# Gathers moved from the start of a stage into the stage before it, with weights and small engine steps re-ordered, in a graph network on one core

## Time and profile before

| | us |
|---|---|
| median of 3 runs | 6474.08 |
| lowest and highest | 6468.80, 6482.52 |
| the profiled execution | 6475.1 |
| its span on the core | 6473.4 |
| busy: PE, DVE, ACT, POOL | 3347.9, 4132.0, 1517.7, 4139.2 |
| mean granted clock of TensorE | 0.675 of full |

### The profile page before, as it was taken

One profiled execution on the slowest core, in us unless ns is written; L12 is line 12 of the kernel. 1 busy time (PEld: TensorE's weight loads), 2 busy tenths in 40 slices (PEclk: granted clock), 3 DMA queues, 4 the chain that ended last, 5 costly groups with the idle time before them and its releaser, 6 DMA issues. The chain is left out here.

```text
span 6473.4 us, 52111 instructions
## 1 busy us (share of the span) xinstructions
PE 3347.9 (52%) x13821; PEld 2034.4 (31%) x13823; DVE 4132.0 (64%) x5381; ACT 1517.7 (23%) x3187; POOL 4139.2 (64%) x4234
## 2 busy tenths in 40 slices
PE   3576777755777776573333333333334333333363
PEld 2355555544555555341111111111111111111231
DVE  5577777766777777565555554555554555555597
ACT  0122222201222221012223322222232233222221
POOL 0477777726777775127777776777775777777230
PEclk7677777876776777785555656556656555666686
DMA  0576666627666665463333332333332333333341
GB/s 22 147 205 194 194 197 199 192 78 203 197 200 196 195 196 148 178 193 98 105 105 105 107 105 85 106 105 105 104 106 87 101 105 107 106 105 102 131 153 61
DMA packets 541084, 877.90 MB, mean 136 GB/s; under 512 B 85205, under 2 KB 383297, under 8 KB 532622
## 3 DMA queue, kind: packets, MB, share of 16 engines
q0 software_dynamic: 167776, 479.21, 25.7%
q1 hardware_dynamic: 373032, 395.35, 19.0%
HBM read 553.75 MB, written 320.47 MB: 135 GB/s over the span
## 5 line engine op out<-in xcount | busy, mean ns | idle before, releaser
L1219 POOL DMA_INDIRECT big<-h_tab,big x2352 | 2219.5, 944 | 812.1 <-issue 812.1
L1265 PE MATMUL psum<-big 128*128 128x512 f32 x1176 | 1086.6, 1079 | 1779.2 <-ACT big L1242 1779.0
L633 POOL DMA_INDIRECT big<-kv_tab,big x1664 | 1645.3, 989 | 532.6 <-issue 498.3
L1302 DVE TENSOR_TENSOR psum<-psum,big 128x1024 f32<-128x1024 f32 x294 | 555.7, 1890 | 1337.7 <-DMA big<-h_tab,big 1337.7
L1265 PEld LDWEIGHTS psum<-big 128*128 128x128 f32 x1176 | 342.7, 322 | 2358.6 <-ACT big L1242 2055.1
L1236 ACT COPY big<-big 128x1024 f32<-128x1024 f32 x294 | 563.5, 1917 | 2097.0 <-DVE big L1285 2097.0
L762 PE MATMUL psum<-big 128*128 128x136 f32 x3328 | 691.6, 358 | 502.7 <-DVE big L820 316.2
L762 PEld LDWEIGHTS psum<-big 128*128 128x128 f32 x3328 | 592.5, 250 | 598.4 <-issue 569.7
L672 ACT COPY big<-psum 125x128 f32<-125x128 f32 x1408 | 375.8, 267 | 1478.2 <-PE psum L718 1394.1
L1285 DVE TENSOR_TENSOR_SCAN big<-big,psum 128x1024 f32<-128x1024 bf16 x294 | 669.0, 2275 | 0.1
L710 PE MATMUL psum<-big 128*128 x4992 | 581.2, 263 | 105.3 <-DVE big L791 105.0
(11 more groups left out here) (391 smaller groups left out, 3315.8 us busy)
## 6 DMA issues: line engine op xcount, KB each, us to landing
run_tab<-big SPq DMA_DIRECT2D x294, 512.0 KB, 2.7
snap_tab<-big SPq DMA_DIRECT2D x176, 448.0 KB
item_tab<-big SPq DMA_DIRECT2D x208, 272.0 KB
big<-loc_tab SPq DMA_DIRECT2D x104, 512.0 KB, 4.6
big<-h_tab,big POOLq DMA_INDIRECT x2352, 2.5
big<-kv_tab,big POOLq DMA_INDIRECT x1664, 3.4
snap_tab<-big SPq DMA_DIRECT2D x176, 52.0 KB
kv_tab<-big SPq DMA_DIRECT2D x12, 512.0 KB, 2.6
```

Source lines behind the costliest of these rows:

```text
L633: nc.gpsimd.indirect_dma_start(out=kv[:, b % SLOTS, k, :], out_offset=None, in_=kv_tab, in_offset=bass.IndirectOffsetOnAxis(ap=src_item[:, ...
L1219: nc.gpsimd.indirect_dma_start(out=got[j % RING][:, k * D:(k + 1) * D], out_offset=None, in_=h_tab, in_offset=bass.IndirectOffsetOnAxis(ap ...
L1265: ins_ = nc.tensor.matmul(bank[2 * (j % DEEP) + k][:, :], ea_T[j % DEEP], w_blocks[:, k * 512:(k + 1) * 512], start=True, stop=True)
L1302: nc.vector.tensor_tensor(by_feature(msg[j % DEEP]), by_feature(msg[j % DEEP]), got[j % RING].rearrange("p (t f) -> p f t", f=D), ALU.add) ...
```

## The change

It touches the first seven stages of the list above:

- `node_linear` and `node_math` are replaced by one stage per layer, `conv_linear`: keys and values are multiplied for all tiles first, two tiles to a bank, then queries and roots; the weights have two semaphores. In the second layer the joins of `node_math` run in it quad by quad, ACT applying the ReLU on its copy. When the table is written, POOL issues the gathers of batches 0 to 2 (`FIRST`) there.
- `conv_finish` makes its one-hots ahead of DVE's first wait (an index tile that they need is made at the end of `conv_edges`), and adds `x` to `skip` in the second layer; `norm_linear` (1) has no L1453 any more.
- `norm_linear` (1) and (3) have POOL issue the first 8 count rows (`EARLY`); `by_src` begins with the ninth. In all three, ACT takes the root of a quad ahead of the next quad's squares, and DVE scales the variance ahead of the next join.
- The four loads of `norm_linear` (2) are issued in `by_src` on `x` instead. Some buffers change places for this.

The diff, cut to its core, each level of indentation shortened to one space:

```diff
+  kv_ring = area(B1, 4 * SLOTS * 2 * D).rearrange("p (b k c) -> p b k c", k=4, c=2 * D)
+  def kv_rows(b, slot_in):
+   for k in range(4):
+    nc.gpsimd.indirect_dma_start(
+     out=kv_ring[:, b % SLOTS, k, :], out_offset=None, in_=kv_tab,
+     in_offset=bass.IndirectOffsetOnAxis(ap=src_item[:, 4 * b + k:4 * b + k + 1], axis=0)).then_inc(slot_in[b % SLOTS], 16)
...
+      for b in range(FIRST, BATCHES):
        if b >= SLOTS:
         pool.wait_ge(va_done, b - SLOTS + 1)
-       for k in range(4):
-        nc.gpsimd.indirect_dma_start(
-         out=kv[:, b % SLOTS, k, :], out_offset=None, in_=kv_tab,
-         in_offset=bass.IndirectOffsetOnAxis(ap=src_item[:, 4 * b + k:4 * b + k + 1], axis=0)).then_inc(slot_in[b % SLOTS], 16)
+       kv_rows(b, slot_in)
...
+      if layer == 1:
+       nc.vector.tensor_tensor(skip[:, :], skip[:, :], x[:, :], ALU.add)
       link_(nc.vector.memset(gT, 0.0))
+      side_hots(0)
+      side_hots(1)
       dve.wait_ge(from_pe, 1)
...
       nc.vector.engine_nop().then_inc(to_act, 1)
-      dve.wait_ge(made, 1)
-      side_hots(0)
       dve.wait_ge(from_act, 2)
...
       nc.vector.engine_nop().then_inc(to_pe, 1)
-      side_hots(1)
       dve.wait_ge(from_pe, 2)
...
+  FIRST = 3
+  def conv_linear(layer, source, slot_in, scale_of=None, joined=None):
+   groups = [[(lo, min(lo + 2, hi)) for lo in range(first_, hi, 2)] for first_, hi in QUADS]
+   pairs = [p for g in groups for p in g]
...
+     ph, "kv_w_in", "qs_w_in", "node_step", "joined_done", "tr_done", "copied", "mm_done", "evac", "tab_out")
...
     with nc.Block() as block:
+     @block.gpsimd
+     def _(pool):
+      pool.wait_ge(tab_out, 16 * len(QUADS))
+      for b in range(FIRST):
+       kv_rows(b, slot_in)
      @block.sync
      def _(sp):
...
+      for k, (n, loaded) in enumerate((("k", kv_in), ("v", kv_in), ("q", qs_in), ("s", qs_in))):
+       sp.dma_start(wgt[:, k * D:(k + 1) * D], a[f"L0_{n}_w{layer}"]).then_inc(loaded, 16)
+       sp.dma_start(bias[:, k * D:(k + 1) * D], a[f"L0_{n}_b{layer}"].to_broadcast([P, D])).then_inc(loaded, 16)
...
+      for g, (lo, hi) in enumerate(QUADS):
+       seen += len(groups[g])
+       sp.wait_ge(evac, seen)
+       sp.dma_start(table(kv_tab)[:, lo:hi, :], kv_n3[:, lo:hi, :]).then_inc(tab_out, 16)
+      sp.wait_ge(qs_in, 16 * 4)
...
+       nc.scalar.activation(turned[:, lo * D:hi * D], bank[g % 2][:, 0:(hi - lo) * D], ACT.Relu if layer else ACT.Copy).then_inc(copied, 1)
      @block.tensor
      def _(pe):
       def turn(g):
        lo, hi = QUADS[g]
+       if joined is not None:
+        pe.wait_ge(joined_done, g + 1)
        later(pe, copied, g - 1)
        for t in range(lo, hi):
         ins_ = nc.tensor.transpose(bank[g % 2][:, (t - lo) * P:(t - lo + 1) * P], source[:, t * D:(t + 1) * D], ident[:, :])
        ins_.then_inc(tr_done, 1)
+      def products(q, at):
+       lo, hi = pairs[q % many]
+       if q >= 6:
+        pe.wait_ge(evac, outs_at(q - 6))
+       for t in range(lo, hi):
+        ins_ = nc.tensor.matmul(bank[2 + q % 6][:, (t - lo) * 2 * D:(t - lo + 1) * 2 * D], turned[:, t * D:(t + 1) * D], wgt[:, at:at + 2 * D], start=True, stop=True)
+       ins_.then_inc(mm_done, 1)
       turn(0)
...
+      pe.wait_ge(kv_in, 16 * 4)
+      q = 0
+      for g in range(len(QUADS)):
        if g + 1 < len(QUADS):
         turn(g + 1)
        pe.wait_ge(copied, g + 1)
...
+       for _ in groups[g]:
+        products(q, 0)
+        q += 1
+      pe.wait_ge(qs_in, 16 * 4)
+      for q in range(many, 2 * many):
+       products(q, 2 * D)
      @block.vector
      def _(dve):
...
+      link = Chain(dve, step)
+      def kv_out(q):
+       lo, hi = pairs[q]
+       dve.wait_ge(mm_done, q + 1)
...
+      if scale_of is not None:
+       scale_of(link)
+      q = 0
+      for g in range(len(QUADS) + 2):
+       if joined is not None and g < len(QUADS):
+        joined(link, *QUADS[g], work3)
+        nc.vector.engine_nop().then_inc(joined_done, 1)
+       if g == 1:
+        dve.wait_ge(kv_in, 16 * 4)
+       for _ in groups[g - 2] if g >= 2 else ():
+        kv_out(q)
+        q += 1
+      dve.wait_ge(qs_in, 16 * 4)
+      for q in range(many, 2 * many):
+       lo, hi = pairs[q - many]
+       dve.wait_ge(mm_done, q + 1)
...
+       for dst, at in ((q_n3, 0), (skip3, D)):
+        nc.vector.tensor_tensor(dst[:, lo:hi, :], out[:, :, at:at + D], bias[:, 2 * D + at:3 * D + at].unsqueeze(1).to_broadcast([P, hi - lo, D]), ALU.add).then_inc(evac, 1)
...
+  R, EARLY = 9, 8
+  counts = [area(k * NP, NP) for k in range(R)]
+  def count_rows(v, cin):
+   at = NT + v if v < 5 else v - 5
+   nc.gpsimd.indirect_dma_start(out=counts[v % R], out_offset=None, in_=snap_tab,
+          in_offset=bass.IndirectOffsetOnAxis(ap=own_at[:, at:at + 1], axis=0)).then_inc(cin[v % R], 16)
...
+     @block.gpsimd
+     def _(pool):
+      for v in range(EARLY if counts_to else 0):
+       count_rows(v, counts_to)
      @block.sync
      def _(sp):
...
       for n in range(last + 1):
+       if n > 0:
+        lo, hi = QUADS[n - 1]
+        act.wait_ge(varied, n)
+        nc.scalar.activation(root[:, lo:hi], var[:, lo:hi], ACT.Sqrt).then_inc(rooted, 1)
        if n < last:
         lo, hi = QUADS[n]
         act.wait_ge(centre, n + 1)
...
        if n > 0:
         lo, hi = QUADS[n - 1]
-        act.wait_ge(varied, n)
-        nc.scalar.activation(root[:, lo:hi], var[:, lo:hi], ACT.Sqrt).then_inc(rooted, 1)
...
       for n in range(last + 3):
+       if 0 < n <= last:
+        spread_of(n - 1)
        if n < last:
         centred(n)
-       if 0 < n <= last:
-        spread_of(n - 1)
        if n >= 3:
         product_out(n - 3)
        if 0 < n <= last:
...
+  conv_edges(1, conv_in)
+  conv_finish(1)
+  norm_linear([(wgt[:, 0:D], a["L1_WT"][0:D, :]), (wgt[:, D:2 * D], a["L1_WT"][D:2 * D, :]), (bias[:, 0:D], a["L1_b"].to_broadcast([P, D]))],
+     node_sums, work3, shares, counts_to=mean_in)
...
     with nc.Block() as block:
      @block.gpsimd
      def _(pool):
-      for v in range(NT + 5):
+      for v in range(EARLY, NT + 5):
        later(pool, mm_done, v - R + 1)
-       at = NT + v if v < 5 else v - 5
-       nc.gpsimd.indirect_dma_start(out=counts[v % R], out_offset=None, in_=snap_tab,
-              in_offset=bass.IndirectOffsetOnAxis(ap=own_at[:, at:at + 1], axis=0)).then_inc(cin[v % R], 16)
+       count_rows(v, cin)
      @block.sync
...
-       sp.wait_ge(we_in, 16 * 10)
+       sp.dma_start(wgt[:, 0:D], a["L2_W_enc"]).then_inc(we_in, 16)
+       sp.dma_start(bias[:, 0:D], a["L2_b_enc"].to_broadcast([P, D])).then_inc(we_in, 16)
+       sp.dma_start(bn[:, :], a["L2_bn"]).then_inc(we_in, 16)
+       sp.dma_start(epsb[:, 0:3], a["L2_eps"].to_broadcast([P, 3])).then_inc(we_in, 16)
+       sp.wait_ge(we_in, 16 * 14)
      @block.vector
...
-  norm_linear([(wgt[:, 0:D], a["L2_W_enc"]), (bias[:, 0:D], a["L2_b_enc"].to_broadcast([P, D])),
-        (bn[:, :], a["L2_bn"]), (epsb[:, 0:3], a["L2_eps"].to_broadcast([P, 3]))], plus_x,
+  norm_linear([], plus_x,
...
+  gat_in = dma_sems(*[f"gat_in{k}" for k in range(R)])
   norm_linear([(wgt[:, 0:D], a["L3_WT"]), (bias[:, 0:D], a["L3_b"].to_broadcast([P, D])),
         (a12[:, 0:D], a["L3_a"][:, 0:D].to_broadcast([P, D])), (a12[:, D:], a["L3_a"][:, D:].to_broadcast([P, D])),
-        (lnwb[:, 0:D], a["L3_ln_w"].to_broadcast([P, D])), (lnwb[:, D:], a["L3_ln_b"].to_broadcast([P, D]))], plus_x, work3)
-  hh = area(0, NPF)
+        (lnwb[:, 0:D], a["L3_ln_w"].to_broadcast([P, D])), (lnwb[:, D:], a["L3_ln_b"].to_broadcast([P, D]))], plus_x, work3, counts_to=gat_in)
+  hh = area(8 * NPF, NPF)
```

## The result

The changed kernel takes **6399.12 us** (median of 4 runs, 6395.10 to 6406.73) beside 6473.39 for the kernel before: a ratio of 0.9885, 95% interval [0.9873, 0.9898]. The forecast was 6406, 6378 to 6436. The profiled execution of the changed kernel took 6406.73, its span is 6404.6, 68.8 shorter than the span before; -68.3 was forecast on that scale. On this pair of executions the sum is right to half a microsecond; its terms are not.

A forecast was written before the change was run, and what follows sets the result against it. No engine was taken to bound the kernel throughout; stages were read singly, waits for counts opening both by_src the main prize. Terms of -85.3 plus 17 gave -68.3 from 6475.1, or 6406 us against the median; range 6378 to 6436.

The forecast's parts named there:

- the start of both by_src: by_src on x and on skip: count rows arrive during the stage before, removing DVE's first waits; -31.3 and -22.9 us.
- the encoder's loads: norm_linear (2): loads land under by_src, so PE's 17.13 us wait goes; with the root's order -17.4 us.
- The first attention stage: First layer's attention stage: PE bounds keys and values, table lands at 206.4, stage ends with POOL's twelfth gather; +3.5 us.
- The second stage: Second layer's attention stage: joins go quad by quad, then table and gathers; -6.4 us, bounds -8 and -2.
- POOL's early gathers: Attention stages: 12 gathers at 1.25 us each, 15.1 us; no gain counted in conv_edges.
- the wait of 12.12: conv_edges, batch 14: POOL waits 12.12 us for a slot that DVE's work frees, so earlier gathers only wait longer.
- the rival with 4%: conv_edges: POOL is the bound after all, early gathers count in full, -15 us per layer, 6375 us; 4%.
- the new wait in norm_linear (3): norm_linear (3): six weight loads queue with the count rows, PE waits at its first product; +17 us, +10.5 to +23.
- No hold: norm_linear (3): small loads slip through within 11 us, stage takes 31.3 us; -85 in all, 6389 us; 25%.
- conv_edges and the gine layers, put at 0: conv_edges and three GINE layers: no step touched, so no change counted, though moved buffers and DMA traffic might lengthen conv_edges.
- The rule of the Trainium skill: norm_linear (3): DMA engines alternate queues, draining one whole packet each turn; by it the hold nears the lower end, +12.
- The clock rival: by_src on x: TensorE's clock stays at 1.2 GHz after idle, 25 steps 5.4 us longer, +135, 6541 us; 3%.

The follow-up runs named there:

- experiment 3: Changed kernel with no count rows issued before by_src (0 in both norms): 6444.07 us, +45 against the changed kernel.
- experiment 5: Changed kernel with the encoder's four loads issued in norm_linear (2) again: 7434.66 us on a slower chip; norm_linear (2) 49.5 instead of 33.6.
- experiment 7: Changed kernel with the root behind the next quad's squares and variance scaling behind the next join again, all three norms: 7444.51 us on a slower chip.
- experiment 1: Changed kernel without gathers ahead of conv_edges (FIRST = 0): 6379.21 us, 0.9849 to the kernel before.
- experiments 9 to 12: Three variants of the changed kernel and, third, that kernel again, on a chip where the kernel before takes 7600.99: 7493.79, 7483.72, 7486.93, 7482.23 us.
- experiment 8: Changed kernel with norm_linear (3)'s six loads issued only after the first count row landed: 7440.00 us on a slower chip; stage 60.5 instead of 39.1.
- 4: Changed kernel without gathers ahead of conv_edges, and with five count rows in norm_linear (3), three in the scores' stage: 6376.59 us, 0.9848 to the kernel before.
- 6: Changed kernel with seven count rows in norm_linear (1), five in (3), none in the scores' stage: 7421.28 us on a slower chip.
- 9: Changed kernel without gathers ahead of conv_edges, seven count rows in norm_linear (1), six in (3): 7493.79 us, 0.9865 to the kernel before.
- experiment 2: Changed kernel with five count rows in norm_linear (3) and three in the scores' stage: 6398.92 us, no difference from the changed kernel.
- experiment 10: Changed kernel without early gathers, count rows 7 and 6, PE and DVE awaiting only two loads in norm_linear (3): 7483.72 us, 0.9843 to the kernel before.
- 12: Changed kernel with x added per quad in norm_linear (1) again, not in conv_finish: 7482.23 us on a slower chip.

## Why the prediction was right, and where it was not

The range, the direction and the size held, mostly because the two large terms did: the start of both by_src (-30.3 and -23.0 of -31.3 and -22.9; experiment 3 puts them back at +31.2 and +22.9) and the encoder's loads (-18.1 of -17.4; experiment 5: 15.9 from the loads, experiment 7: 2.8 from the root, for which the prediction's 17.4 leaves about 1 beside PE's wait of 17.13).

**The first attention stage** came out at +3.8 of +3.5 by luck: two errors cancel. The table had landed at 203.9 and not 206.4. PE started at 185.71 and not 186.9. A quad's products and transposes follow each other in 2.16 us and not 2.4. And the stage doesn't end with POOL's twelfth gather, as the prediction has it, but 3.2 us later. The second stage (-3.4 of -6.4) likewise ends 2.6 us after its twelfth gather; there the table landed where it was put, within 1.

**POOL's early gathers** bring nothing to conv_edges on the first chip, as argued from the wait of 12.12 (experiment 1). On the chip of experiments 9 to 12, by two executions of each sort, the layers with them are some 14 us shorter, for the 9 to 10 that they cost; the four layers of each sort spread by 10 and 22 us. That is the size the rival with 4% named, but not its mechanism: POOL bounds conv_edges less there, as it waits 337 us and more for slots.

**The step that failed is the new wait in norm_linear (3).** The prediction put it at PE's first product, with +17. The six loads are issued from 5991.98 to 5994.31, the first row at 5993.84, and the rows' data flows only from 5998.6. By then 793 of the 864 packets of SP's queue have started, so nearly all loads land ahead of the rows (6.2 us for the last, not 24.6). The sum put 32 of the loads' 48 packets per engine behind or between the rows; it left out the 4.8 us from the first gather's issue to its data, which stood only in the rival *No hold*. Those 4.8 us are no fixed latency: in norm_linear (1), whose three loads are nearly through by then, and in experiment 8, where the loads come later, they are 1.6. So the loads in front seem to hold the rows back, and not the rows the loads. It is a race. In experiments 1, 4, 5, 6 and 9 the rows' data begins 2.5 to 3.4 us after the issue, the last load lands about with the first row, and PE waits 3.7 to 4.3; in the changed kernel (both executions) and in 2, 7, 10 and 12 it begins 4.1 us or more after, and PE waits 0.8 to 1.0. What tips it isn't settled. The wait that is there stands at the stage's end: a block is not left before its gathers have landed, and the instruction that waits is POOL's DRAIN. It takes 10.8 us in (3), 1.5 in (1), and about 3 in each attention stage. Experiment 2 shows it by row count, experiments 3 and 6 again. Net, norm_linear (3) came out at +4.8 and not +13.6: its own work is 5.7 shorter (forecast 3.4; the cycle fell from 4.79 to 3.61 and not to 3.87, as PE's next transposes start 1.87 us after its products and not 2.08; experiment 7 gives back exactly the 5.7), and the hold adds 10.5.

That this term was 8.8 too high is not seen in the sum because conv_edges and the gine layers, put at 0, together came out 7 longer in this execution. On the first chip gine_nodes takes 47 or 51 us from one layer to the next in every kernel, at a granted clock of 0.82 or 0.74, and the two conv_edges of its six profiled executions sum up to 2253 to 2259: no step of the change. So the agreement to half a microsecond is luck. The profiled execution was the slowest of the four, 7.6 above the median, which is why the forecast meets it and lies 6.9 above the median.

The rule of the Trainium skill that the prediction weighed ("DMA: Bandwidth & Descriptors", section "Queues, rings and completion order": turns between queues, a whole packet of one at a time) is borne out in kind by experiment 8, where loads and rows truly meet: 4.5 us for each 64 KB load. By it alone, an estimate: a turn of one row's share (8 x 0.49 = 3.9 us) per load gives 20 us for five loads; 22.4 were measured.

The clock rival had 3% and didn't come: the granted clock is 0.97 over by_src on x, from its first difference on.

## What to carry to other kernels

Work that is issued ahead into a stage with a barrier at its end isn't free there: count when its last byte lands against the stage's own end, and issue only as many rows as fit. Small loads that the stage itself needs have to be through before the bulk's data flows, or they pay for it packet by packet (experiment 8); those needed first get a semaphore of their own (experiment 10). A stage that lives on a small round trip through HBM is the wrong place for bulk (experiment 2). Before prefetching into a ring, read the first wait for a slot: if it is there already, a sooner issue may only lengthen it, as on the first chip. On another chip the same edit came out otherwise, so try it on more than one.

## What the hardware showed that was not expected

- A block's end waits for POOL's indirect DMAs though no semaphore in the program asks for it: 10.79 us with eight rows, 0.32 with five. It is POOL's DRAIN at the block's end, 34.7 us with eight rows, 24.3 with five, 0.05 with none.
- The same kernels take 16 to 17% longer on two of the three chips, all of it in conv_edges, conv_finish, gine_edges and gine_nodes; the cause is open. The change is worth more there: 0.9843 [0.9825, 0.9861] or 114 us on one of them, 0.9885 [0.9873, 0.9898] or 74 us on the first. Where the other 40 us lie can't be said, as the kernel before has no trace there.
- A POOL gather of 1.6 MB has its data flowing 1.6 us after its issue in norm_linear (1), and 2.5 to 4.8 us in (3) with six small loads issued just ahead; with the loads behind the rows (experiment 8) it is 1.6 in (3) too.
- Where small packets and packets of 12.8 KB are queued together, they pass one for one (601 and 602 in 18 us), so a small packet costs its load about the time of a large one: 0.56 us, and 0.49 for a large one at 417 GB/s.
